# Four chained layers on one core: a mixture layer that reads tiles ahead of its stores, and decay-scan sums made by adding transfers

## The reference

```python
decay = exp(-exp(w)) * (0.5 + 0.5 * tf)            # per feature and batch
ek, ekv = exp(min(k, 30)), exp(min(k, 30)) * v
# forward and backward recurrences over the 256 positions: a = a * decay + e
nf, df = scan(ekv), scan(ek)
nb, db = scan(ekv, reverse), scan(ek, reverse)
euk = exp(min(u + k, 30))
num = nf + nb - ekv + euk * v
den = df + db - ek + euk
out = sigmoid(r) * (num / max(den, 1e-8)) * (0.8 + 0.2 * tf)
```

## Time and profile before

| | us |
|---|---|
| median of three runs | 1016.86 |
| the profiled execution, its own time | 1019.41 |
| its span, first to last instruction | 1017.7 |
| busy PE / DVE / ACT / POOL | 786.0 / 592.2 / 384.1 / 236.5 |
| layer 0, feed-forward part | from 115 to 182.5 |
| layer 1 up to the first turned tile | 182.5 to 224.2 |
| layer 1, tile loop | 224.2 to 326 |
| layer 1, gather and sum | 326 to 346 |
| layers 2 and 3 | 346 to 1017.7 |

### The profile page before, as it was taken

How to read it: one execution, slowest core, us unless ns; L and a number is a source line. 1 busy time by engine, 2 the same in 40 slices (tenths; PEclk the granted TensorE clock), 3 DMA queues, 4 the chain that set the end, 5 groups by cost and what they waited for, 6 DMA issues and landing times. The chain is left out here.

```text
span 1017.7 us, 11188 instructions
## 1 busy us (share of the span) xinstructions
PE 786.0 (77%) x3629; PEld 588.3 (58%) x3629; DVE 592.2 (58%) x1268; ACT 384.1 (38%) x832; POOL 236.5 (23%) x216
## 2 busy tenths in 40 slices
PE   0776557656556625659999999999986999999995
PEld 0332435523233411448888788888876788888884
DVE  6889699369878377644655655555553333333333
ACT  2300512212122258645454454454453333343332
POOL 0401000140100347022012012012001255554543
PEclk9887778578988759869999999999996899999998
DMA  4000000731111500030010010100002231314321
GB/s 132 0 2 0 1 0 1 298 120 31 32 31 37 187 4 1 1 124 9 34 43 5 38 42 1 43 0 2 1 1 63 75 104 52 104 52 104 94 48 41
DMA packets 37374, 49.85 MB, mean 49 GB/s; under 512 B 18670, under 2 KB 30038, under 8 KB 35654
## 3 DMA queue, kind: packets, MB, share of 16 engines
q1 hardware_dynamic: 36262, 46.90, 14.8%
q0 software_dynamic: 768, 2.10, 0.6%
q10 hardware_dynamic: 288, 0.14, 0.1%
HBM read 43.00 MB, written 6.13 MB: 48 GB/s over the span
## 5 line engine op out<-in xcount | busy, mean ns | idle before, releaser
L2029 DVE TENSOR_TENSOR B_l<-bank,TW_l 128x512 f32<-128x512 f32 (+1 forms) x50 | 34.6, 692 | 140.8 <-PE bank L1974 140.8
L1648 ACT ACTIVATE EX<-EX,nm 128x128 f32<-128x128 f32 (+1 forms) x128 | 57.2, 448 | 108.5 <-DVE nm L1697 107.9
L1598 POOL TENSOR_TENSOR WL<-RAW,WH 128x512 fp32r<-128x512 f32 x32 | 41.1, 1290 | 231.6 <-ACT WH L1622 231.6
L2064 POOL TENSOR_TENSOR HL_l<-H_l,HH_l 128x512 fp32r<-128x512 f32 (+1 forms) x50 | 64.1, 1283 | 119.9 <-ACT HH_l L2043 119.9
L1974 PE MATMUL bank<-XH,WH_l 128*128 128x512 f32 (+1 forms) x200 | 79.8, 399 | 0.0
L1974 PE MATMUL bank<-XL,WH_l 128*128 128x512 f32 (+1 forms) x200 | 79.5, 398 | 0.0
L1974 PE MATMUL bank<-XH,WL_l 128*128 128x512 f32 (+1 forms) x200 | 79.5, 398 | 0.0
L134 POOL TENSOR_TENSOR WV<-EUK,V 128x512 f32<-128x512 f32 x16 | 23.5, 1475 | 178.4 <-DVE GAIN L219 178.4
L1711 DVE TENSOR_TENSOR AL<-bank,AH 128x256 fp32r<-128x256 f32 x64 | 27.1, 424 | 62.1 <-ACT AH L1663 62.1
L1751 PE MATMUL bank<-XH,WH 128*128 128x512 f32 x128 | 59.5, 465 | 3.9 <-DVE XL L1454 3.9
L2051 ACT ACTIVATE S_l<-bank 128x512 f32<-128x512 f32 (+1 forms) x50 | 30.1, 601 | 83.9 <-PE bank L1974 83.9
(11 more groups left out here) (307 smaller groups left out, 2089.9 us busy)
## 6 DMA issues: line engine op xcount, KB each, us to landing
RAW<-l_attn SPq DMA_DIRECT2D x8, 1024.0 KB, 5.0
WE<-l_experts SPq DMA_DIRECT2D x1, 6144.0 KB, 19.8
RAW_l<-l_experts SPq DMA_DIRECT2D x9, 512.0 KB, 3.9
TW_l<-routed SPq DMA_DIRECT2D x16, 256.0 KB, 5.2
RAW<-l_w SPq DMA_DIRECT2D x3, 1024.0 KB, 7.2
TW_l<-routed SPq DMA_DIRECT2D x14, 192.0 KB, 3.2
RAW_l<-l_experts SPq DMA_DIRECT2D x9, 256.0 KB, 4.7
sorted_x<-ZERO SPq DMA_DIRECT2D x1, 1920.0 KB, 24.4
```

The lines of the kernel that those rows point to most:

```text
L1598: pool.tensor_tensor(WL[:, slot, c], RAW[:, slot, c], WH[:, slot, c].bitcast(F32), ALU.subtract).then_inc(w_low, 1)
L1648: act.activation(EX[:, s, a:b], EX[:, s, a:b], ACT.Exp, bias=nm[:, s, i:i + 1], scale=scale, accum_out=rs[:, s, i:i + 1]).then_inc(expd, 1)
L2029: v.tensor_tensor(self.B[0:rows, q % 2], self.k.banks[2 * (q % 2) + 1][0:rows], self.TW[0:rows, w % self.TWS, n * W:(n + 1) * W], ALU.mult ...
L2064: pool.tensor_tensor(self.HL[0:rows, q % 4], self.H[0:rows, q % 2], self.HH[0:rows, q % 4].bitcast(F32), ALU.subtract).then_inc(self.h_low, 1)
```

## The change

Four things change. (1) The `add` piece of chunks 4 to 15 leaves DVE. POOL queues four transfers a chunk that add their source to their destination in on-chip memory, 128x512 float32 each: first DB onto DF and NB onto NF; when both have landed, EUK onto DF and WV onto NF. POOL waits for the first two before it queues the others. The division waits for the last two (`g_all`). (2) DF, DB, NF and NB of these chunks take turns between two slots, where they had one. The order of pieces becomes den, num of chunk c, then divide of chunk c-1. Layer 0 has one piece a step (12), layer 1 has two before the first logits are waited for, one behind HOT, four beside the shared expert, one a tile (15), and two behind the loop (24). (3) In layer 1, SP loads six tiles ahead of the first store and then tile j+6 before the store of tile j (`load` still waits until the tile three before has been turned), and the zeros are written ahead of the experts' weights. (4) PE does the rank products ahead of the shared expert's first product, and no longer waits for `g_done` near the end of layer 1.

```diff
+def gain_queue(pool, k, c):
+    layer, j = gain_layer(c)
+    slot = gain_slot(c)
+    n = c - gain_sum_no(c)
+    pool.wait_ge(k.g_scan, 8 * c + 8)
+    pool.dma_start(k.DF[slot][:], k.DB[slot][:], accum_op=ALU.add).then_inc(k.g_both, 16)
+    pool.dma_start(k.NF[slot][:], k.NB[slot][:], accum_op=ALU.add).then_inc(k.g_both, 16)
+    pool.wait_ge(k.g_both, 32 * n + 32)
+    pool.wait_ge(k.g_w, c + 1)
+    pool.dma_start(k.DF[slot][:], chunk(k.EUK[layer][:], j), accum_op=ALU.add).then_inc(k.g_all, 16)
+    pool.dma_start(k.NF[slot][:], k.WV[:, c % 2], accum_op=ALU.add).then_inc(k.g_all, 16)
...
-            v.wait_ge(k.g_add, 4 * (c - gain_sum_no(c)) + 4)
+            v.wait_ge(k.g_all, 32 * (c - gain_sum_no(c) + 1))
...
+def gain_pieces(first, last):
+    for c in range(first, last + 1):
+        if c < last:
+            yield c, "den"
+            yield c, "num"
+        if c > first:
+            yield c - 1, "divide"
...
+            sp.wait_ge(made, 1)
+            sp.dma_start(xs_d.rearrange("(j p) d -> p j d", p=P),
+                         ZERO[:].rearrange("p (o d) -> p o d", o=1).to_broadcast([P, TILES1, D])).then_inc(zeroed, 16)
             sp.dma_start(WS[:], io["l1_experts"][0]).then_inc(ws_in, 16)
...
-            for j in range(RING1):
+            for j in range(2 * RING1):
                 load(j)
             for j in range(TILES1):
-                if j + RING1 < TILES1:
-                    load(j + RING1)
+                if j + 2 * RING1 < TILES1:
+                    load(j + 2 * RING1)
...
             for c in range(FIRST_GAIN1, FIRST_GAIN1 + 2):
                 gain_pool(pool, k, c)
+            gain_queue(pool, k, FIRST_GAIN1)
             pool.wait_ge(zeroed, 16)
...
+            gain_queue(pool, k, FIRST_GAIN1 + 1)
             for c in range(FIRST_GAIN1 + 2, LAYERS * NCH):
                 gain_pool(pool, k, c)
+                gain_queue(pool, k, c)
             for n in range(RING1):
                 pool.wait_ge(y_out[n], 16 * len(range(n, TILES1, RING1)))
```

More of the change, by code:

```diff
@@ L191, in num_scans @@
         self.both_ways(self.k.EKV, self.k.NF[self.slot], self.k.NB[self.slot])
[L193 to L205, removed]
     def divide(self, den=None, num=None):
@@ L220, in divide, with gain_pieces_done @@
                                ALU.min, ALU.mult).then_inc(k.g_done, 1)
+def gain_pieces(first, last):
[5 more added lines that the diff above has]
+            yield c - 1, "divide"
+def gain_pieces_done(v, k, pieces):
+    for c, what in pieces:
+        g = GainVector(v, k, c)
+        if what == "den":
+            g.den_scans()
+        elif what == "num":
+            g.num_scans()
+        else:
+            g.divide()
 ORDER = [0, 2, 1, 3]
@@ L406, in _ @@
                 gain_pool(pool, k, c)
+                if not gain_summed(c):
+                    gain_queue(pool, k, c)
         @block.scalar
@@ L597, in low @@
                                 ALU.subtract).then_inc(hlo, 1)
-            def gain_piece(n):
-                GainVector(v, k, NCH + n // 4).piece(n % 4)
+            pieces = list(gain_pieces(NCH, 2 * NCH))
             for q in range(NPAIR):
@@ L612, in _ @@
                     low(q - 1)
[L613 to L617, removed]
+                gain_pieces_done(v, k, pieces[q:q + 1])
             low(NPAIR - 1)
@@ L719 @@
 FIRST_GAIN1 = 2 * NCH
[L722 to L730, removed]
+PIECES = list(gain_pieces(FIRST_GAIN1, LAYERS * NCH))
+LOGITS1, RANKS1, START1, MIDDLE1, END1 = 2, 1, 4, 15, 2
+FIRST_PIECE2 = LOGITS1 + RANKS1 + START1 + MIDDLE1 + END1
 def pieces_after(j):
-    left = len(PIECES1) - STEPS1
-    return PIECES1[STEPS1 + left * j // TILES1:STEPS1 + left * (j + 1) // TILES1]
+    at = LOGITS1 + RANKS1 + START1
+    return PIECES[at + MIDDLE1 * j // TILES1:at + MIDDLE1 * (j + 1) // TILES1]
 def layer1(nc, k, io):
@@ L961, in _ @@
             v.tensor_scalar(EID[:], which[:], float(E1 - 1), float(WCOLS1), ALU.min, ALU.mult).then_inc(pos, 1)
-            def piece(c, what):
-                g = GainVector(v, k, c)
-                if what == "den":
-                    g.den_scans()
-                elif what == "num":
-                    g.num_scans()
-                elif what == "add":
-                    g.add()
-                else:
-                    g.divide()
-            for q in range(STEPS1):
+            gain_pieces_done(v, k, PIECES[at:at + START1 - 4])
+            at += START1 - 4
+            for q in range(4):
                 v.wait_ge(s_silu, q + 1)
                 v.tensor_tensor(HS[:, q], SS[:, q % 2], shared_banks[q % 2][1][:], ALU.mult).then_inc(s_h, 1)
-                piece(*PIECES1[q])
+                gain_pieces_done(v, k, PIECES[at + q:at + q + 1])
             for j in range(TILES1):
@@ L984, in _ @@
                 v.tensor_tensor(HT[:, j % 2], ST[:, j % 2], banks[j % 2][:, F1:2 * F1], ALU.mult).then_inc(h, 1)
-                for c, what in pieces_after(j):
-                    piece(c, what)
+                gain_pieces_done(v, k, pieces_after(j))
+            gain_pieces_done(v, k, PIECES[FIRST_PIECE2 - END1:FIRST_PIECE2])
         @block.tensor
@@ L1023, in _ @@
             mm.then_inc(hot_sum, 1)
+            pe.wait_ge(ws_in, 16)
+            shared_up(0)
             pe.wait_ge(xtok, 4)
```

19 lines of the change are left out of this document (8 added, 11 removed).

## The result

The changed kernel takes 985.48 us (median; 982.11 to 987.56, four runs) beside 1018.44 us (1016.75 to 1020.51, four runs) for the kernel before: a ratio of 0.967, 95% interval 0.964 to 0.971, or 33 us less. The forecast was 968.5 us with a range of 954 to 995, so the time lies in the range, 17 us above the forecast and 1.5 us above the sum's own upper bound of 984. A second measurement beside the experiments gave 983.34 us and 0.962 (0.958 to 0.965).

A forecast was written before the change was run, and what follows sets the result against it. DVE was taken to bound layer 0's feed-forward part, and PE's wait for late XIN loads layer 1's loop. Terms -6.3 - 6.4 - 38.3 + 2.6 = -48.4 us from 1019.41 gave 971.0, less 2.55 968.5 us; range 954 to 995.

The forecast's parts named there:

- the sum's own upper bound: Whole kernel: 984 us, with a landing of 5.2 us and four tiles at half clock; the low bound was 957.
- transfers of 5 to 8 us: Rival, adding transfers: a landing of 5 to 8 us gives a time of 984 to 1005 us; chance 0.15.
- half clock: Rival, layer 1's tile loop: PE at half clock throughout, 81 us, total 993; chance 0.12 together with loads still late.
- loads still late: Rival, tile loop: only half of XIN's wait goes, loop about 73 us, total 985; chance 0.12 together with half clock.
- The loop: Layer 1's tiles, HT(0) to HT(14): XIN's wait goes, DVE is next, 94.7 us becomes 56.4, -38.3.
- The clock term: Tile loop: 5.4 us allowed for tiles that PE does at half clock, a choice below the 9 us of four tiles.
- Layer 0: Feed-forward part: four add pieces go (-10.1 us), waits of 0.9 and 2.9 come, sum -6.3.
- The wait of chunk 4: Layer 0: a chain of 9.3 us against 8.4 of cover makes DVE wait 0.9 us before the division.
- Start of layer 1: Up to the first load: scatters begin at 204.1 instead of 208.70 and take 10.1 us, -6.4.
- End of layer 1: Behind the last HT: the gather waits behind chunk 15's transfers, starting 9.9 us after it instead of 7.3, +2.6.
- The landing: Each adding transfer of 256 KB on POOL's queue: 3.4 us to land, with bounds of 2.0 and 5.2.
- transfers slower than any row: Rival: adding may cost more than any row; at a 9 us landing, chain 20.5 us, the gain is gone.

The follow-up runs named there:

- no_products: The changed kernel with POOL's products WV of chunks 5 to 15 left out, EKV added instead (sums not the reference's): 975.58 us, 0.955.
- plain_copies: The changed kernel with accum_op left out of a chunk's four transfers, so they copy and don't add (sums missing): 964.79 us, 0.943.
- gap: The changed kernel with a third WV buffer and the next chunk's product issued between the two pairs of transfers: 973.56 us, 0.953.
- chunk8_dve: The changed kernel with the four additions of chunk 8 (first of layer 1) back on DVE: 980.80 us, 0.960.
- reads_alone: The kernel before with only the loads issued six tiles ahead, additions still on DVE: 1007.34 us, 0.984.
- chunk15_dve: The changed kernel with the four additions of chunk 15 (last of layer 1) back on DVE: 978.99 us, 0.957.
- adds_alone: The changed kernel with the loads three tiles ahead, as before the change: 1039.61 us, 1.018.
- zeros_late: The changed kernel with the zeros stored behind the experts' weights again, as in the kernel before: 987.06 us, 0.967.

## Why the prediction was right, and where not

**The number.** The forecast was 48.4 us less than before, and it is 33. The time is in the range of 954 to 995, but not in the sum's own bounds, 957 to 984, and it falls where I had put transfers of 5 to 8 us, half clock or loads still late. None of these was there: the pairs landed in 3.4 and 4.7 us (medians), PE's wait for XIN was gone and the clock in the loop was 0.96. What missed are terms of the sum, named below: three stages with the same sign, 15 us together. That the range held them owes more to its width than to the sum.

**The loop (-38.3, measured -39.7): right in size, in another mixture.** That PE's wait for XIN would go and DVE be next was right, and both halves alone show it: the reads without DVE's relief stop at 82.3 us, and DVE's relief without the reads doesn't help at all. The sum had 46.0 us of DVE's work, 5.0 for scans beside WV and 5.4 for PE's clock. In the trace four scans between HT(0) and HT(14) are stretched by 1.8 to 2.0 us each, 7.5 in all, and reciprocals wait 0.95 and 0.99 us: 46.0 + 7.5 + 1.9 = 55.4, against 55.1. The clock term was not needed; it is 0.96 between the two HT, where I allowed a quarter of the time at half, and what PE lost by it lay beside DVE. (The price itself was off too: the up product of 3.38 us that I took for half clock had 0.58 granted. Between 224.2 and 231, at 0.51, one took 3.78. And four tiles at 2.1 more are 8.4 us, not 9.) So the sum had 4.4 us too little for scans and waits and 5.4 too much for the clock. The two errors met, and that the loop came out within 1.4 us is luck in part. In the second trace of the changed kernel no reciprocal waits there, and the loop takes 52.8 us.

**Layer 0 (-6.3, measured -0.1): the term left out was the product on POOL.** By rows: 10.1 us of additions gone, three scans stretched by 2.3, 1.9 and 2.3 us, and 4.0 us of wait for chunk 7, makes +0.4. In the kernel before the product had stretched two subtractions HL by 0.7 us each, 1.4 that went too, so the rows come to -1.0 and 0.9 us stays unexplained. The wait was forecast at 2.9; the chain of two pairs measured 10.3 us from the end of the scans, not 9.3, against a cover of 6.35 us for which I had 6.4. The wait of chunk 4 (0.9) did not come: the stretched scans ahead of its division covered it, and without the product (`no_products`) it is 2.40 us. The earlier trace rows showed a scan of 1.68 us beside WV, and I put that into the loop only and kept its size; in layer 0 I put it at nothing, though the rows above show the product at work there. But the stretch is not a fixed price. The scan ends some 0.55 us behind the product, in the earlier trace rows and in the changed kernel alike, so it costs what is left of the product when the scan begins. The change issues WV directly behind the second pair, which puts it at a scan's start, and its record is 1.93 us, where before it was 1.27 in layer 0 and 1.70 beside the scans of the loop. It begins before the issue ahead of it has ended (130.76, with that issue from 130.19 to 131.40), and with the short issues of `plain_copies` it is 1.26 to 1.31 again; that the overlap lengthens it is argued from that. That the product stretches the scans `no_products` and `gap` show, by taking it away and by moving it.

**Start of layer 1 (-6.4, measured -0.9): the landing of chunk 8's first pair.** I took 6.3 us from the row of `COND` and it is 11.5. That alone is 5.2 us; the issue ahead of it took 0.6, not 1.26, and the first scatter comes 4.4 us behind the forecast. The other 1.1 us of the 5.5 lie between the first load and HT(0). `plain_copies`, with the pair landing 3.6 us sooner (185.27 to 193.16, 7.9 us), puts the first scatter at 21.5 us behind the first X, which is the place of the forecast (204.1 less 182.68 is 21.4); `chunk8_dve` at 20.5. The eight scatters did take the 10.1 us that I gave them (205.84 to 215.90), 1.8 less than before, which fits the additions on DVE as what had stretched one of them; in `reads_alone`, which keeps the additions there, one scatter takes 3.32 us beside all four. The rule that I had set against that row (the Trainium skill, "SBUF — State Buffer", Who interferes with whom) would have kept the 1.7 us; the trace of the changed kernel has no scatter over 1.10 us, and sides with the row. The first load then takes 10.0 us to HT(0), not 8.9.

**End of layer 1 (+2.6, measured +6.0).** That the gather would wait behind chunk 15's transfers was right, and `chunk15_dve` shows it. It starts at 11.9 us, not 9.9: one more stretched scan (2.26 us at 282.79, +1.6) and 0.5 us in the landing. From the first gather to layer 2 it takes 14.6 us instead of 13.1. Chunk 15's second pair is still on its way then, but with it gone (`chunk15_dve`) it takes 15.1 us, so the cause of this last 1.5 us stays open.

**The landing.** I took 3.4 us with 2.0 and 5.2 as bounds; the rows have 3.4 for DF<-DB and 4.7 for NF<-NB, which ends the pair. The page figure that I had set beside it (the Trainium skill, "DMA: Bandwidth & Descriptors", Anatomy of one DMA, SWDGE path, an estimate of 2.6 us) fits the copies, 2.5 and 2.8 us in `plain_copies`, and not the adding ones. The issues were priced too high: the second transfer of a pair is issued 0.57 us behind the first, not 1.26. So a pair takes 5.2 us from its first issue to its landing, where I had 4.66, and the two errors took off from one another. The adding is a price of its own, and the rival "transfers slower than any row" was right in kind, at 10 us for a chain and not 20.

**Layers 2 and 3 (0, measured +4.3).** The instructions there are the same. The thirteen other traces have 673.2 to 676.2 us here, `reads_alone` too (676.1), and only the trace of before has 671.6; the granted clock is 0.93 there and 0.92 in the changed kernel. Whether the layers really take 2 to 4 us more when they start at another moment, or that one execution was a short one, stays open; `reads_alone`, whose program there is that of before, speaks for the second.

## What to carry to other kernels

Work moved to an engine or a queue that looks idle is paid where nothing covers it: count the chain at each end of a layer by itself, and leave the first and the last piece where it was (here 8.5 us more). A relief of one engine is worth nothing while a ring of load, compute and store sets the pace: `adds_alone` lost 18 us with less work on DVE, and the same additions gained as soon as the loads were early. Where an instruction of VectorE meets a product on GpSimd, move the product to a place beside a reciprocal; such a stretch in the trace of before is to be re-priced for the new place, not copied.

## What the runs showed of the hardware that I had not expected

- A transfer of 256 KB within on-chip memory that adds costs twice the engine time of one that copies: with 48 of them the queue has 8.1% of 16 engines and 7680 packets, against 4.2% and 4608. GpSimd's issues of a pair take 0.87 and 1.21 us instead of 0.55 to 0.59.
- While they run, other transfers land later: YO's stores 3.1 us instead of 1.7, XIN 3.2 instead of 2.2 (medians). With the copies it is 1.7 and 2.3. It takes a full loop: in `adds_alone`, where the same adding transfers are spread over twice the time (DMA share 0.37, not 0.67), it is 1.7 and 2.2.
- Beside a 6 MB load of weights, the first pair of adding transfers took 11.5 us, the copies 7.9, and the weights themselves 25.8 and 26.1 us. Without this chunk's transfers (`chunk8_dve`) they took 23.0, with the zeros behind them (`zeros_late`) 21.8.
- A scan or a subtraction on VectorE that meets GpSimd's product of two operands ends some 0.55 us behind it (2.26 to 3.01 us instead of 0.67 for the scans of the changed kernel); a reciprocal beside the same product is not held (3.35 us in both cases).
- With less work for DVE and the same late loads, TensorE's granted clock in the loop fell from 0.89 to 0.75, and the kernel with less work on DVE was the slower one. What made the clock fall was not tried by itself.
